# Two-layer adaLN program with top-1 experts: combining inside the second projection, experts in skewed order, attention's early loads one unit at a time

## The reference

```
x [8 batches, 512 tokens, 128 channels]; mod = silu(c) @ wmod -> shifts, scales, gates, one set for each layer
layer 0: h = layernorm(x) * (1 + ca) + sa
         x = x + ga * causal_attention(h)              16 heads of 8, one shared key and value head, rotary
         h = layernorm(x) * (1 + cb) + sb
         x = x + gb * top1_experts(h)                  8 experts, 128 -> 512 -> 128, capacity 640 rows each
layer 1: h = layernorm(x) * (1 + ca) + sa
         x = x + ga * attention(h)                     q and k divided by their norms, no mask
         h = layernorm(x) * (1 + cb) + sb
         x = x + gb * local_transformer(h)             two small layers with windows of 64
```

## Time and profile before

| | us |
|---|---|
| median of three runs | 2201.26 |
| lowest and highest | 2190.42, 2208.6 |
| the profiled execution, its own time | 2199.45 |
| its span, first to last instruction | 2197.5 |

### The profile page before, as it was taken

How to read it: one execution, slowest core, us unless ns; L and a number is a source line. 1 busy time by engine, 2 the same in 40 slices (tenths; PEclk the granted TensorE clock), 3 DMA queues, 4 the chain that set the end, 5 groups by cost and what they waited for, 6 DMA issues and landing times. The chain is left out here.

```text
span 2197.5 us, 41648 instructions
## 1 busy us (share of the span) xinstructions
PE 1783.0 (81%) x12612; PEld 925.7 (42%) x12676; DVE 1361.1 (62%) x2370; ACT 1170.7 (53%) x2826; POOL 908.7 (41%) x1063
## 2 busy tenths in 40 slices
PE   7559999957077284699999975589999999999996
PEld 4324444425066163133333323255555555555552
DVE  5557777713011332588888832578878888878872
ACT  2226766731033043277777760267767777767671
POOL 5424445421500554001111101376766766666660
PEclk9769999975599586599999995699999999999996
DMA  4312222210122112022222212011111111111110
GB/s 129 108 51 73 79 82 79 75 38 0 48 91 80 38 43 84 33 82 79 88 80 85 77 57 104 21 39 39 35 36 32 47 38 36 32 37 32 46 34 12
DMA packets 93680, 126.46 MB, mean 58 GB/s; under 512 B 17040, under 2 KB 56851, under 8 KB 93456
## 3 DMA queue, kind: packets, MB, share of 16 engines
q1 hardware_dynamic: 91536, 121.11, 17.5%
q0 software_dynamic: 2048, 4.16, 0.6%
HBM read 66.28 MB, written 43.52 MB: 50 GB/s over the span
## 5 line engine op out<-in xcount | busy, mean ns | idle before, releaser
L968 DVE TENSOR_REDUCE M_sb<-banks 128x1 f32<-128x512 f32 (+3 forms) x1024 | 539.3, 583 | 186.4 <-PE banks L768 100.1
L854 ACT ACTIVATE probs_sb<-banks 128x512 f32<-128x512 f32 (+3 forms) x1024 | 469.4, 521 | 191.7 <-PE banks L794 187.7
L765 PE MATMUL banks<-K_sb,Q_sb 72*128 72x512 bf16 (+3 forms) x1024 | 360.3, 358 | 49.1 <-PEq L310 40.4
L794 PE MATMUL banks<-Q_sb,K_sb 75*128 75x512 bf16 (+3 forms) x1024 | 345.4, 344 | 6.8 <-ACT probs_sb L854 3.9
L809 PE MATMUL banks<-probs_sb,V_sb 128*32 128x512 f32 (+3 forms) x2048 | 233.5, 527 | 12.0 <-issue 7.7
L1793 ACT ACTIVATE l_p_sb<-banks,l_nb_sb,l_inv_sb 128x128 f32<-128x128 f32 x512 | 228.4, 466 | 12.9 <-DVE l_nb_sb L1965 12.7
L765 PEld LDWEIGHTS banks<-K_sb,Q_sb 72*128 72x128 bf16 x1024 | 100.7, 99 | 301.0 <-DVE M_sb L968 171.8
L1879 POOL TENSOR_TENSOR l_pn_sb<-l_p_sb,l_rs_sb 128x512 f32<-128x512 f32 x128 | 147.9, 1156 | 154.4 <-DVE l_rs_sb L1971 152.3
L1871 POOL TENSOR_TENSOR l_inv_sb<-l_clip_sb,l_minus_half_sb 128x16 f32<-128x16 f32 x64 | 186.3, 2911 | 56.7 <-DVE l_clip_sb L1940 54.8
L1864 POOL TENSOR_TENSOR l_ts_sb<-l_t_sb 128x1024 f32<-128x1024 f32 x64 | 153.4, 2397 | 36.9 <-DVE l_kn_sb L1949 21.0
L794 PEld LDWEIGHTS banks<-Q_sb,K_sb 75*128 75x128 bf16 x1024 | 99.9, 99 | 93.4 <-ACT probs_sb L854 20.1
(11 more groups left out here) (204 smaller groups left out, 3377.2 us busy)
## 6 DMA issues: line engine op xcount, KB each, us to landing
Q_sb<-qk_dram SPq DMA_DIRECT2D x192, 96.0 KB
o_dram<-osum_sb SPq DMA_DIRECT2D x64, 256.0 KB, 4.9
l_vs_sb<-l_vt_sb SPq DMA_DIRECT2D x112, 128.0 KB, 2.3
qk_dram<-parts_sb SPq DMA_DIRECT2D x96, 128.0 KB
K_sb<-qk_dram SPq DMA_DIRECT2D x32, 288.0 KB
opack_sb<-o_dram SPq DMA_DIRECT2D x16, 256.0 KB, 3.4
inverse_sb<-s_dram SPq DMA_DIRECT2D x16, 256.0 KB, 3.3
ew_sb<-in_ew SPq DMA_DIRECT2D x16, 256.0 KB, 2.9
```

The costliest lines, as they stand in the source:

```text
L765: mm = pe.matmul(out[:, 0:width], g.Q[0:RK, slot, h, k * P:(k + 1) * P], g.K[0:RK, slot, hk(h), 0:width], start=True, stop=not causal)
L794: pe.matmul(SB[ring % 3][:, t0:N], g.K[0:RM, q, hk(h), k * P:(k + 1) * P], g.Q[0:RM, q, h, t0:N], start=True, stop=True).then_inc(s["b_sco ...
L854: act.activation(g.probs[:, k, h, t0:N], SB[ring % 3][:, t0:N], ACT.Exp, scale=scale)\
L968: dve.reduce_max(g.M[:, u % 2, k, h:h + 1], SA[ring % 3][:, 0:width], AX.X, negate=True)\
```

## The change

Three edits. (1) The block `combine` is gone. Its gathers, gate products, transpositions and additions are instructions of `project(g, 1)`, which begins one step earlier (`lo - 3`); batch `it+3` is combined in step `it`, its rows are gathered by POOL at the end of step `it-2`, and the multiplication by `gb` and the addition are one instruction. The transposition writes the bank that v uses. In layer 1 both remainders of q and k go from POOL to DVE: that of q to the end of its step, that of k into the next step. (2) `experts` is written out over all eight experts, with three buffers for loads (and their rows in a tile of their own). PE transposes the next expert's rows between the hidden layer and the answers of this one. (3) In both layers the three units' loads are issued one at a time, ahead of the stores of batches `lo + 3`, `lo + 4` and `lo + 5`. `std` and `rstd` are gone, `route` uses `ra` in their place, and `setup_experts` is called ahead of the first projection.

```diff
+def combine_gather(g, pool, b):
+    s = g.gs
+    if b >= 2:
+        pool.wait_ge(s["picked"], b - 1)
+    for t in range(b * CH, (b + 1) * CH):
+        pool.indirect_dma_start(g.htok[:, t, :], None, g.answers,
+                                bass.IndirectOffsetOnAxis(ap=g.slot_out[:, t:t + 1], axis=0))\
+            .then_inc(g.gathered[b % 2], 16)
+def combine_pick(g, dve, b):
+    s = g.gs
+    at = slice(b * CH, (b + 1) * CH)
+    dve.wait_ge(g.gathered[b % 2], (b // 2 + 1) * CH * 16)
+    dve.wait_ge(s["pturned"], b)
+    dve.tensor_tensor(g.xc[:, :].rearrange("p (c n) -> p c n", c=CH), g.htok[:, at, :],
+                      g.gate_w[:, at].unsqueeze(2).broadcast_to([P, CH, C]), ALU.mult).then_inc(s["picked"], 1)
+def combine_turn(g, pe, b, kept):
+    s = g.gs
+    pe.wait_ge(s["picked"], b + 1)
+    pe.wait_ge(s["x2"], b)
+    pe.wait_ge(g.ps["v_kept"], kept)
+    for c in range(CH):
+        mm = pe.transpose(g.bank[6][:, c * P:(c + 1) * P], g.xc[:, c * P:(c + 1) * P], g.ident[:, :])
+    mm.then_inc(s["pturned"], 1)
+def combine_add(g, dve, b):
+    s = g.gs
+    dve.wait_ge(s["pturned"], b + 1)
+    dve.scalar_tensor_tensor(out=g.x[:, b, :], in0=g.bank[6][:, :], scalar=g.mod[:, 5, b:b + 1], in1=g.x[:, b, :],
+                             op0=ALU.mult, op1=ALU.add).then_inc(s["x2"], 1)
 def project(g, layer):
-    steps = range(lo - 2, hi + 1)
+    steps = range(lo - 2 - layer, hi + 1)
...
-                    for u in range(3):
-                        load_unit(g, sp, layer, lo, u)
+                if lo + 3 <= it < lo + 6:
+                    load_unit(g, sp, layer, lo, it - lo - 3)
...
+                else:
+                    pe.wait_ge(g.gs["x2"], it - lo + 1)
                 norm_mean(g, pe, it + base, it - lo)
...
             def project_v(it):
                 pe.wait_ge(s["v_kept"], it)
+                if layer == 1:
+                    pe.wait_ge(g.gs["x2"], min(it - lo + 3, B))
...
                     if inside(it):
                         spread_norms(it, 1)
+                    if inside(it + 3):
+                        combine_turn(g, pe, it + 3 - lo, max(it + 1, lo))
...
             if layer == 0:
                 start_gpsimd(g, pool)
+            else:
+                combine_gather(g, pool, 0)
+                combine_gather(g, pool, 1)
             for it in steps:
...
                 if inside(it + 2):
                     norm_power(g, pool, it + 2 + base)
-                if layer == 1 and inside(it):
-                    remainder(it, 0)
-                if inside(it):
+                if layer == 0 and inside(it):
                     remainder(it, 1)
+                if layer == 1 and inside(it + 5) and it + 5 >= lo + 2:
+                    combine_gather(g, pool, it + 5 - lo)
...
+            def remainder(it, w):
+                dve.wait_ge(s["part1"], it * 2 + w + 1)
+                dve.wait_ge(s["part3"], it * 2 + w - 1)
+                dve.tensor_tensor(g.res[:, w, :], g.qk[:, 2 * (it % 2) + w, :], g.parts[:, it % 2, w, 0, :],
+                                  ALU.subtract).then_inc(s["res1"], 1)
...
                     if inside(it + 1):
                         finish(it + 1)
+                    if inside(it - 1):
+                        remainder(it - 1, 1)
                     if inside(it + 2):
                         norm_center(g, dve, it + 2 + base, it + 2 - lo)
                     if inside(it):
                         keep_v(it)
+                    if inside(it + 3):
+                        combine_pick(g, dve, it + 3 - lo)
+                    if inside(it):
                         over_norm(it, 0)
                     if inside(it + 2):
                         norm_epsilon(g, dve, it + 2 + base)
                     if inside(it):
                         over_norm(it, 1)
+                        remainder(it, 0)
+                    if inside(it + 3):
+                        combine_add(g, dve, it + 3 - lo)
...
+            def load(e):
+                at, sem = e % 3, g.eload[e % 3]
+                sp.dma_start(rows_in(e), g.slots_by_expert[e]).then_inc(sem, 16)
+                sp.dma_start(g.ew1[:, at, :], g.ins["ew1"][e]).then_inc(sem, 16)
+                sp.dma_start(g.eb1[:, at, :], g.ins["eb1"][e]).then_inc(sem, 16)
+                sp.dma_start(g.ew2[:, at, :].rearrange("p (f c) -> p f c", c=C), g.ins["ew2"][e]).then_inc(sem, 16)
+                sp.dma_start(g.eb2[:, at, :], g.ins["eb2"][e]).then_inc(sem, 16)
+
+            load(0)
+            load(1)
+            for e in range(E):
+                if e + 2 < E:
+                    if e:
+                        sp.wait_ge(s["biased"], e * ST)
+                    load(e + 2)
+                sp.wait_ge(s["biased"], (e + 1) * ST)
+                sp.dma_start(g.answers_by_expert[e], tile(ys[e % 2])).then_inc(g.estored[e % 2], 16)
+            for slot in range(2):
+                sp.wait_ge(g.estored[slot], E // 2 * 16)
...
+            def turn_rows(e):
+                pe.wait_ge(g.eload[e % 3], (e // 3 + 1) * 80)
+                pe.wait_ge(s["xT"], e * 2)
+                for t in range(ST):
+                    bank, col = (g.bank[0], t * P) if t < 4 else (g.bank[1], 0)
+                    mm = pe.transpose(bank[:, col:col + P], rows_in(e)[:, t, :], g.ident[:, :])
+                mm.then_inc(s["turned"], 1)
+
+            def hidden(e):
+                pe.wait_ge(s["xT"], e * 2 + 2)
+                for f in range(F // P):
+                    for half in range(2):
...
+            def answer(e):
+                pe.wait_ge(s["relu"], (e + 1) * HT)
+                for t in range(ST):
+                    if e * ST + t >= 2:
+                        pe.wait_ge(s["biased"], e * ST + t - 1)
+                    bank = g.bank[6 + (e * ST + t) % 2]
...
+            turn_rows(0)
+            for e in range(E):
+                hidden(e)
+                if e + 1 < E:
+                    turn_rows(e + 1)
+                answer(e)
...
+            def copy_turned(e):
+                dve.wait_ge(s["turned"], e + 1)
+                dve.wait_ge(s["hidden"], e * HT)
+                dve.tensor_copy(g.exT[:, 0:512], g.bank[0][:, :]).then_inc(s["xT"], 1)
+                dve.tensor_copy(g.exT[:, 512:CAP], g.bank[1][:, 0:CAP - 512]).then_inc(s["xT"], 1)
+
+            copy_turned(0)
+            for e in range(E):
+                if e + 1 < E:
+                    copy_turned(e + 1)
+                if e >= 2:
+                    dve.wait_ge(g.estored[e % 2], e // 2 * 16)
+                for t in range(ST):
+                    dve.wait_ge(s["answer"], e * ST + t + 1)
+                    dve.tensor_tensor(tile(ys[e % 2])[:, t, :], g.bank[6 + (e * ST + t) % 2][:, 0:C],
+                                      g.eb2[:, e % 3, :], ALU.add).then_inc(s["biased"], 1)
 
```

More of the change, by code:

```diff
@@ L1016, in setup_experts @@
         "setup", "sq", "turned", "htok", "lpsum", "logits",
-        "vec", "counts", "scattered", "picked", "pturned", "pscaled", "x2")}
+        "vec", "counts", "scattered", "picked", "pturned", "x2")}
+    g.gathered = [g.sem(f"g_gathered{i}") for i in range(2)]
 def gate(g):
@@ L1199, in setup_expert_loop @@
 def setup_expert_loop(g):
-    g.ew1 = g.sb("ew1", [P, 2, F])
-    g.ew2 = g.sb("ew2", [P, 2, F])
-    g.eb1 = g.sb("eb1", [P, 2, F // P])
-    g.eb2 = g.sb("eb2", [P, 2, C])
+    g.ew1 = g.sb("ew1", [P, 3, F])
+    g.ew2 = g.sb("ew2", [P, 3, F])
+    g.eb1 = g.sb("eb1", [P, 3, F // P])
+    g.eb2 = g.sb("eb2", [P, 3, C])
+    g.exs = g.sb("exs", [P, 3, CAP])
     g.eh = g.sb("eh", [P, F // P, CAP])
     g.exT = g.sb("exT", [P, CAP])
-    g.es = {n: g.sem("e_" + n) for n in ("turned", "xT", "hidden", "relu", "answer", "biased", "stored")}
-    g.eload = [g.sem(f"e_loaded{i}") for i in range(2)]
+    g.es = {n: g.sem("e_" + n) for n in ("turned", "xT", "hidden", "relu", "answer", "biased")}
+    g.eload = [g.sem(f"e_loaded{i}") for i in range(3)]
+    g.estored = [g.sem(f"e_stored{i}") for i in range(2)]
 def experts(g):
@@ L1233, in two @@
-            def two(i, last):
-                for par in range(2):
-                    if par == 0:
-                        sp.wait_ge(s["answer"], i * 2 * ST)
-                        load(i * 2 + 1, 1)
-                    sp.wait_ge(s["biased"], (i * 2 + par + 1) * ST)
-                    sp.dma_start(g.answers_by_expert[i * 2 + par], tile(ys[par])).then_inc(s["stored"], 16)
-                    if par == 0 and not last:
-                        load(i * 2 + 2, 0)
-            load(0, 0)
@@ new lines, in turn_rows @@
+            def turn_rows(e):
[9 more added lines that the diff above has]
+                    for half in range(2):
+                        n = f * 2 + half
+                        if e * HT + n >= 4:
+                            pe.wait_ge(s["relu"], e * HT + n - 3)
+                        pe.matmul(g.bank[2 + n % 4][:, 0:HALF], g.ew1[:, e % 3, f * P:(f + 1) * P],
```

(13 more changed lines are left out.)

111 lines of the change are left out of this document (11 added, 100 removed).

## The result

The changed kernel takes 2138.28 us, the median of 4 runs (2136.26 to 2139.61); the kernel before took 2199.79 (2190.42 to 2208.6) beside it. The ratio is 0.9716, with a 95% interval of 0.9694 to 0.9737: 61.5 us less. The forecast was 2156. The profiled execution took 2139.61 us, with a span of 2137.9.

The account below looks back on a forecast made before the run. Bounds: PE's order in the experts; in the second projection the PE-POOL chain, then a full queue from the third batch's first store. 2199.45 less 20.3, 25.0 and 0 is 2154.2; median 1.8 above, so 2156; range 2134 to 2180.

Parts of the forecast that it names:

- the stall: Second projection: ACT's 18.8 us wait before `first_part` for a store to `qk_dram`, claimed to be a full queue.
- rival A: Both projections: spreading the loads gives back the stall's 18.8 us and the first projection's 16.7, so 2120; chance 0.15.
- Experts, -20.3 us: Experts: the next expert's transpositions fill the wait for relus; cycle 10.0 us instead of 12.9, seven cycles save 20.3.
- The lower bound, 5.19 + 4.54: Experts: cycle if nothing is added, hidden start to answers 5.19 plus 4.54, given as 9.8 us; bound of 21.7 us saved.
- Start of the second projection, T = 30.8: Second projection, T counted from the first gather: first `power` at T = 30.8, 34.0 us earlier than before.
- Steps with gathers, 13.3 us: Second projection: three steps with gathers take 13.3 us each, the middle of 11.7 and 15, giving back 9.0 us.
- POOL bound of 11.7: Steps with gathers at best: `power` to `norm_power` end 6.4, gathers 5.0, gaps 0.3; this bound gives -29.8 us.
- PE at 1.2 GHz throughout, 15: Steps with gathers at worst: PE falls to 1.2 GHz, 14.5 us, with waits 15; this bound gives -19.9 us.
- The stretch of the full queue, 78.8 us: Second projection, third batch's first store to the end: the queue moves the same stores and loads, 78.8 us.
- Loads one unit at a time, 0 us: Both projections: the waits move and shrink, the bytes stay, 0 us; first projection from -5 to +2.
- about 128: Second projection's end, in us behind the first gather, if the queue were faster and computing decided it.
- Contention, 0: Second projection: gathers, 2.11 MB beside the stores, cost 0 us, given DMA shares 0.17 and 0.24 and early issue.

Follow-up runs that it names:

- e1: The changed kernel with the three units of attention's loads issued at once again: 2141.17 us, ratio 0.9733 to the kernel before.
- e3: The kernel before with only the loads of attention issued one unit at a time: 2192.96 us, ratio 0.9971 to the kernel before.
- e5: The changed kernel with two of a step's four gathers issued ahead of `norm_power`, two behind: 2133.64 us, ratio 0.9705 to the kernel before.
- e4: The changed kernel with `qk_dram` laid out part first, each store one run of 128 rows, six loads a unit: 2083.64 us, ratio 0.9465 to the kernel before.
- e2: The kernel before with only the new order of experts (`setup_expert_loop` and `experts` of the changed kernel): 2167.33 us, ratio 0.985 to the kernel before.

## Why the prediction was right, and where it was not

**What bounds the kernel.** That the stall is a full queue, worth nothing by itself, held: rival A's 35 us against the 2 to 3 of e1 and e3. But "the queue is full" was only half the reading. The share of 0.24 stood in the earlier trace rows, and I used it to say that there was room for the gathers, not to ask why a quarter of the engines was all that a full queue could keep busy. The forecast didn't need it; the next 55 us did.

**Experts, -20.3 us:** measured -22.2. The mechanism held (transpositions under the relus, copies and additions under the answers, loads in time at 104 GB/s). The mis-sized term is the cycle, 9.66 for 10.0. By the rows it is 4.31 from hidden layer to transpositions, 0.78 to the answers, and 4.57 until the next hidden layer. The prediction added the durations, 4.58, 0.76 and 4.73, and these overlap where one group follows another without a gap. Seven cycles of 0.34 make 2.4 us more than forecast, and 0.5 of it is lost elsewhere in the stage. (The lower bound, 5.19 + 4.54, is 9.7 and not 9.8.)

**Start of the second projection, T = 30.8:** measured 28.7. The first mean came at T = 9.0 (9.1). The second `norm_power` ended at 23.5 for 25.0: of the two transpositions that I added in full, the second batch's (706.54) ends 0.49 us before PE's next wait ends, so some of it lies in idle time, and the third batch's (714.31) stands behind the matmuls of the variance that this `norm_power` waits for.

**Steps with gathers, 13.3 us:** measured 13.2, 13.3, 13.3, but that the middle was right is luck. I took it between a POOL bound of 11.7 and PE at 1.2 GHz throughout, 15. The chain is that of the lower bound, gathers behind `norm_power`, only that `power` to the end of `norm_power` takes 8.1 us (720.91 to 728.98) and not 6.4: 8.1 + 5.0 + 0.2 = 13.3. No transposition of the combining lies in between. The 1.7 us are TensorE's clock: the gathers hold `power` back, PE idles 2.92 us, and from 722.9 to 726.7 it runs at 0.56, so that the matmuls from the norm's spreading (L425) to the variance (L248) start 3.8 us apart instead of 2.2 at full clock (792.02 to 794.23 in the kernel before). The two bounds were not alternatives; the one brought on a piece of the other. The earlier trace rows had a hint: the same distance was 7.5 us at 811. e5 moves half of the gathers and shows both parts.

**The stretch of the full queue, 78.8 us:** measured 75.6, at the same bytes (6.53 MB for 6.55). e1 and e3 say that some 2 us of the 3.2 are the spread loads: **Loads one unit at a time, 0 us** was off by that much in the second projection; in the first it held. The prediction also gave the end without a slow queue, "about 128" behind the first gather; e4 measures 122.0 (788.64 - 666.61).

**Contention, 0:** held, and the reason given held too: all gathers were issued before the third batch's first store (the last at 759.8, the store at 763.8, T = 71.6). The other reason, shares of 0.17 and 0.24 that are together well under 1, was none: at 0.24 the stores' four engines were full.

**The whole:** the sum of the steps was -45.3 and the spans give -59.6. 1.9 of the 14.3 is the experts, 5.4 the projection (2.1 at its start, 3.2 in the full queue), and 7.0 come from what the change doesn't touch: the local transformer's 8.9 and 0.8 ahead of the experts, less 2.7 in the second attention. So nearly half of what the forecast missed is luck of that kind. The other 3 us between 2156 and 2138.28 lie between runs and profile: I added 1.8 for a median above the profiled run, and the changed kernel's median is 1.3 below it.

## To carry to other kernels

When a DMA queue looks full, look at the share of the DMA engines beside its rate. Here 86 GB/s at 0.24 came from transfers laid over a quarter of the engines: spreading the loads or giving them to another queue moved 0 to 3 us, while making the slowest dimension of the stores large gave 55. A wait that is long because of what stands ahead in a queue is priced by what the queue would otherwise have carried, not by its length. Once one kind of transfer is made quick, the slow ones beside it cost more than before (3 against 11 us here). An engine that idles in the middle of a step and is busy at its end is worth looking at: moving two issues from the end into the idle time gave 6 to 7 us, part of it because TensorE no longer idled and kept its full clock.

## What the runs showed that I had not expected

The local transformer is the same code in all kernels and took 797.0 to 797.6 us in nine of the twelve profiles, but 806.4, 805.4 and 803.3 in the kernel before, e3 and e2. Its granted clock is alike (0.97 to 1.00 in its full windows in e3 and in the changed kernel). In the timeline of the kernel before, in the fourteenth of its sixteen passes (eight batches, two layers):

```profile
2004.52 1.57 DVE L1949 TENSOR_TENSOR l_kn_sb<-l_ts_sb,l_inv_sb 128x512 f32<-128x512 f32 x1
```

In the changed kernel this instruction takes 0.66 us, and 1.11 to 1.22 in eight of 64 places; in the kernel before and in e3 it takes those, and 1.32 to 1.58 in five more, one in each of the last five passes, which follow each other every 46.5 to 48.5 us and not every 46.1. Both are kernels with the old order of experts; e2, with the new one, has none of these five and is still at 803.3, with three passes of 47.5 us in the same region. So the same code can fall into one pattern or another, worth up to 9 us. What chooses it is open; it wasn't tried. It isn't even shown that it belongs to the kernel and not to the single execution: each kernel has one profile, and while the changed kernel's first four runs lie within 3.4 us, those of the kernel before spread over 18, e3's over 16 and e4's, whose profile has 797.6, over 18 too. Part of the skew's 30 us in e2 (22.4 in the stage) and of the change's 61.5 is of this kind, so what the change itself is worth is better read from the stages: 22.2 and 30.4 us.
